# A graph network on Trainium2: 214 instead of 216 groups of tiles in each of three passes over the edges, with the last rounds of some loops written out

## What is computed

```python
def _propagate(h, edge_attr, edge_index, We, be, Wl):       # twice: pass 1 and pass 2
    x_edge = jnp.concatenate([h[edge_index[0]], h[edge_index[1]], edge_attr], axis=-1)
    x_edge = silu(x_edge @ We + be)
    x_edge = edge_attr @ Wl * x_edge
    return _seg_mean(x_edge, edge_index[0], h.shape[0]) + h

# layer 4: pass 3, with src = edge_index[0], dst = edge_index[1]
x_i, x_j = h[src], h[dst] + ee
alpha = leaky_relu((x_i * att_i).sum(-1) + (x_j * att_j).sum(-1))
e = jnp.exp(alpha - segment_max(alpha, src)[src])
alpha = e / (segment_sum(e, src)[src] + 1e-16)
out = segment_sum(x_j * alpha[:, :, None], src).mean(axis=1) + bias
```

## Time and profile before

| | us |
|---|---|
| median of 3 runs | 13832.53 |
| lowest and highest run | 13831.42, 13838.11 |
| the profiled execution | 13845.22 |
| its span, first to last instruction | 13843.5 |
| stage of pass 1, from the span's start | 6580 to 8870 |
| stage of pass 2 | 9050 to 11320 |
| stage of pass 3 | 11410 to 13720 |

### The profile page before, as it was taken

How to read it: one execution, slowest core, us unless ns; L and a number is a source line. 1 busy time by engine, 2 the same in 40 slices (tenths; PEclk the granted TensorE clock), 3 DMA queues, 4 the chain that set the end, 5 groups by cost and what they waited for, 6 DMA issues and landing times.

```text
span 13843.5 us, 199525 instructions
## 1 busy us (share of the span) xinstructions
PE 9124.3 (66%) x43992; PEld 6407.8 (46%) x43993; DVE 7459.0 (54%) x18791; ACT 3827.0 (28%) x8556; POOL 9553.0 (69%) x8478
## 2 busy tenths in 40 slices
PE   0266665776663679897666666766666656667676
PEld 0011112222111345554666666466666655666666
DVE  8876665777761220101343333333343348999998
ACT  0144445444410111111222222222222222333332
POOL 0168887888886766564777777467777757777774
PEclk9999999999996779898555555555555555665665
DMA  9942222222226999799644444244444438999996
GB/s 380 406 90 19 20 19 14 20 20 20 20 14 216 379 354 324 278 325 219 110 106 104 103 103 104 54 97 104 104 105 104 104 82 171 178 177 177 177 179 128
DMA packets 1476698, 1975.29 MB, mean 143 GB/s; under 512 B 1005691, under 2 KB 1023803, under 8 KB 1410045
## 3 DMA queue, kind: packets, MB, share of 16 engines
q1 hardware_dynamic: 744700, 1265.08, 34.4%
q0 software_dynamic: 454160, 346.91, 14.8%
q10 hardware_dynamic: 277362, 357.67, 8.1%
HBM read 1466.26 MB, written 503.63 MB: 142 GB/s over the span
## 4 chain that ended last, share of the span: by engine, by line
POOL 41%; issue 20%; DMA 13%; PE 11%; SPq 7%; DVE 6%; ACT 1%; DVEq 1%; POOLq 0%; ACTq 0%
POOL gat L793 24%; POOL adj L745 14%; DMA b_row<-acc 5%; PE bank L1230 4%; DMA adj<-put_n,put_at 4%; POOL rec_src L731 4%; SPq L684 3%; DMA arena<-adj 2%; SPq L691 2%; DMA rec_src<-pay,ring_i 2%; DVE arena L1585 1%; PE same L1374 1%; PE bank L1118 1%; SPq L679 1%; PE same L1165 1%
## 5 line engine op out<-in xcount | busy, mean ns | idle before, releaser
L793 POOL DMA_INDIRECT gat<-q_table,ring_i x3456 | 3482.4, 1008 | 1368.9 <-issue 1051.5
L745 POOL DMA_INDIRECT adj<-put_n,put_at x1632 | 2558.5, 1568 | 1276.2 <-DVE put_at L1669 660.1
L1396 PE MATMUL bank<-onehot_t,onehot 128*128 128x64 f32 x6912 | 1585.0, 424 | 1424.8 <-DVE acc L1887 973.6
L731 POOL DMA_INDIRECT rec_src<-pay,ring_i x1632 | 1740.1, 1066 | 866.9 <-issue 491.3
L1396 PEld LDWEIGHTS bank<-onehot_t,onehot 128*128 128x128 f32 x6912 | 1507.1, 331 | 1501.7 <-DVE acc L1887 850.9
L793 POOL DMA_INDIRECT arena<-h_table,ring_i x1728 | 1753.6, 1015 | 629.4 <-issue 503.3
L1300 PE MATMUL same<-onehot 32*128 32x512 f16 x3264 | 1680.0, 616 | 620.7 <-DVE onehot L1640 392.8
L1648 DVE TENSOR_SCALAR_CACHE_REDUCE onehot<-same 128x128 bf16<-128x128 f32 (+3 forms) x1632 | 1232.6, 755 | 867.0 <-PE same L1302 816.4
L1386 PE MATMUL bank<-hs,arena 128*128 x6912 | 1565.3, 422 | 89.7 <-ACT arena L1020 89.6
L1386 PEld LDWEIGHTS bank<-hs,arena 128*128 128x128 f32 x6912 | 1525.9, 334 | 92.8 <-issue 92.8
L902 ACT ACTIVATE arena<-iota_lo,arena 128x128 bf16<-128x128 f32 x3264 | 995.8, 387 | 1109.3 <-PE bank L1125 1009.2
(11 more groups left out here) (321 smaller groups left out, 13965.8 us busy)
## 6 DMA issues: line engine op xcount, KB each, us to landing
arena<-adj SPq DMA_DIRECT2D x240, 1280.0 KB
arena<-rec_src SPq DMA_DIRECT2D x3456, 69.0 KB
adj<-hs ACTq DMA_DIRECT2D x25, 6656.0 KB, 46.4
arena<-adj SPq DMA_DIRECT2D x60, 2560.0 KB, 18.1
rec_src<-pay ACTq DMA_DIRECT2D x1, 119232.0 KB, 332.3
arena<-lo_row SPq DMA_DIRECT2D x3456, 32.0 KB
hs<-b_row SPq DMA_DIRECT2D x432, 256.0 KB
acc<-b_row SPq DMA_DIRECT2D x432, 256.0 KB
```

The costliest lines, as they stand in the source:

```text
L731: nc.gpsimd.indirect_dma_start(rec_src, bass.IndirectOffsetOnAxis(ring_i[:, q, u:u + 1], 0), pay[:, q, u, :], None, bounds_check=SLOTS - 1 ...
L745: nc.gpsimd.indirect_dma_start(counts, bass.IndirectOffsetOnAxis(put_at[:, b // 3 % 4, c:c + 1], 0), put_n[:, b // 3 % 4, c:c + 1], None, ...
L793: nc.gpsimd.indirect_dma_start(rows[n][:, u, :], None, table, bass.IndirectOffsetOnAxis(ring_i[:, n, u:u + 1], 0)).then_inc(landed[n], 16)
L1396: last = mm(bank[6 + n % 2][:, u // 2 * D:(u // 2 + 1) * D], onehot[:, n % 2, u, :], msg[n % 2][:, u, :], start=u % 2 == 0, stop=u % 2 == 1)
```

## The change

`NL = 214` is the number of groups that can hold a tile below 1708. All engines stop after group 213 in each pass, and the counts that waits compare with follow: `k * NL` groups of pass 1, and `turns(n)`, the number of groups that used buffer `n`, 54, 54, 53 and 53. `NG`, the memory layout and the tables stay at 216 groups.

The last round no longer has all its groups: two of four in passes 1 and 2 (`REST4`), six of eight in pass 3 (`REST8`). POOL and SP end their loops a round earlier and run these behind the loop as straight code. DVE in passes 1 and 2 ends its loop a round earlier too, and writes out the last full round and the two groups behind it. In pass 3 the sums of the last group, which stood behind the last round on DVE, are now made in it, in the place of the first group that is left out.

```diff
--- before.py
+++ after.py
@@ -35,6 +35,8 @@
 E1, L1 = 10, 10 + D
 RW = 10 + 2 * D
 NG = TT // U
+NL = -(-TMAX // U)
+REST4, REST8 = NL - (NG // 4 - 1) * 4, NL - (NG // 8 - 1) * 8
 OFF = 4
 SPLIT = 8
 TA = 4 * P
@@ -60,6 +62,7 @@
 TQ = TT // 4
 PAIRS = U // 2
 HI_BITS = 6
+assert 0 < REST4 <= 4 and 0 < REST8 < 8 and NL % 2 == 0
 assert FA < FB and 4 * U * (FB + 1) <= TA < TT and NG % 4 == 0
 assert NG % 8 == 0 and NH <= 1 << HI_BITS and PAIRS * HI_BITS <= 24 and TQ <= 512
 PW = HEADS * D + 2 * HEADS
@@ -464,7 +467,7 @@
 
         def live(i, n):
 
-            return not isinstance(i, int) or 0 <= i * 8 + n < NG
+            return not isinstance(i, int) or 0 <= i * 8 + n < NL
 
         def eights(eng, body):
 
@@ -475,6 +478,10 @@
                     body(i, n)
             for n in range(8):
                 body(NG // 8 - 1, n)
+
+        def turns(n):
+
+            return (NL - n + 3) // 4
 
         def nth(i, n, lag=LAG):
 
@@ -640,24 +647,29 @@
             def load_all_edges(k):
                 if k:
                     sp.wait_ge(f_res, NCH * 4)
-                    sp.wait_ge(l_msg, NG + OFF)
-                    sp.wait_ge(l_oht, NG + OFF)
+                    sp.wait_ge(l_msg, NL + OFF)
+                    sp.wait_ge(l_oht, NL + OFF)
                 for n in range(4):
                     load_edges(k, 0, n)
+
+                def freed(i, n):
+                    sp.wait_ge(l_msg, i * 4 + (k * NL + n - 3 + OFF))
+                    sp.wait_ge(l_oht, i * 4 + (k * NL + n - 3 + OFF))
+                    load_edges(k, i, n)
 
                 def more(first, end):
                     with loop(sp, first, end) as i:
                         for n in range(4):
-                            sp.wait_ge(l_msg, i * 4 + (k * NG + n - 3 + OFF))
-                            sp.wait_ge(l_oht, i * 4 + (k * NG + n - 3 + OFF))
-                            load_edges(k, i, n)
+                            freed(i, n)
 
                 if k:
-                    more(1, NG // 4)
+                    more(1, NG // 4 - 1)
                 else:
                     more(1, FB)
                     store_other_digits()
-                    more(FB, NG // 4)
+                    more(FB, NG // 4 - 1)
+                for n in range(REST4):
+                    freed(NG // 4 - 1, n)
 
             store_table(EV_PQ, q_table[0], acc[:])
             store_first_digits()
@@ -795,16 +807,18 @@
                         bass.IndirectOffsetOnAxis(ring_i[:, n, u:u + 1], 0)).then_inc(landed[n], 16)
 
             def node_rows(k, i, n):
-                hold(pool, l_idx, i * 4 + (k * NG + n + 1))
+                hold(pool, l_idx, i * 4 + (k * NL + n + 1))
                 gathers(q_table[k], gat4, l_gat, n)
 
             for k in range(2):
                 pool.wait_ge(d_table, 16 * (1 + k))
                 for n in range(4):
                     node_rows(k, 0, n)
-                with loop(pool, 1, NG // 4) as i:
+                with loop(pool, 1, NG // 4 - 1) as i:
                     for n in range(4):
                         node_rows(k, i, n)
+                for n in range(REST4):
+                    node_rows(k, NG // 4 - 1, n)
 
             def score_rows(i, n):
                 hold(pool, t_idx, nth(i, n))
@@ -813,9 +827,11 @@
             pool.wait_ge(d_table, 16 * 3)
             for n in range(8):
                 score_rows(0, n)
-            with loop(pool, 1, NG // 8) as i:
+            with loop(pool, 1, NG // 8 - 1) as i:
                 for n in range(8):
                     score_rows(i, n)
+            for n in range(REST8):
+                score_rows(NG // 8 - 1, n)
 
 
         @block.scalar
@@ -1008,10 +1024,10 @@
                                    bias=b_mlp[m][:, 0:1]).then_inc(f_act, 1)
 
             def propagate_act(k):
-                G = k * NG
+                G = k * NL
 
                 def distance(i, n):
-                    act.wait_ge(l_lo[n], i * (16 * SPLIT) + (k * (NG // 4) + 1) * 16 * SPLIT)
+                    act.wait_ge(l_lo[n], i * (16 * SPLIT) + (k * turns(n) + 1) * 16 * SPLIT)
                     act.activation(lo_bc[n], lo_bc[n], ACT.Abs, bias=neg_p[:, 0:1]).then_inc(l_abs, 1)
 
                 def onehot_rows(i, n):
@@ -1047,8 +1063,8 @@
                     for b in range(1, 4):
                         digit_rows(b)
                     groups(FA, NG // 4 - 1)
-                for n in range(4):
-                    group(NG // 4 - 1, n, 4 - n)
+                for n in range(REST4):
+                    group(NG // 4 - 1, n, REST4 - n)
 
             layer_act(0, "h", FT[1])
             digit_rows(0)
@@ -1413,8 +1429,8 @@
                     for b in range(1, 4):
                         digit_rows(b)
                     groups(FA, NG // 4 - 1)
-                for n in range(4):
-                    if n < 3:
+                for n in range(REST4):
+                    if n < REST4 - 1:
                         look_up(NG // 4 - 1, n + 1)
                     sums(NG // 4 - 1, n)
 
@@ -1861,9 +1877,9 @@
                     last.then_inc(l_oh, 1)
 
                 def edge_part(i, n):
-                    landed = i * (16 * U) + (k * (NG // 4) * 16 * U + 16 * U)
+                    landed = i * (16 * U) + (k * turns(n) * 16 * U + 16 * U)
                     dve.wait_ge(l_gat[n], landed)
-                    dve.wait_ge(l_pay[n], i * (16 * SPLIT) + (k * (NG // 4) + 1) * 16 * SPLIT)
+                    dve.wait_ge(l_pay[n], i * (16 * SPLIT) + (k * turns(n) + 1) * 16 * SPLIT)
                     v.tensor_tensor(gat4[n], gat4[n], pay4[n][:, :, E1:E1 + D], ALU.add).then_inc(l_q1, 1)
 
                 def node_part(i, n):
@@ -1911,14 +1927,16 @@
                             group(i, n)
 
                 if k:
-                    groups(1, NG // 4 - 1)
+                    groups(1, NG // 4 - 2)
                 else:
                     groups(1, FB)
                     dve.wait_ge(d_tab[1], 16)
-                    groups(FB, NG // 4 - 1)
+                    groups(FB, NG // 4 - 2)
                 for n in range(4):
-                    group(NG // 4 - 1, n, more=False, last=n == 3)
-                gather_sums(NG // 4 - 1, 3)
+                    group(NG // 4 - 2, n, more=n < REST4)
+                for n in range(REST4):
+                    group(NG // 4 - 1, n, more=False, last=n == REST4 - 1)
+                gather_sums(NG // 4 - 1, REST4 - 1)
 
             def residual(j, n, other):
                 for c, (c0_, m) in enumerate(CHUNKS):
@@ -2127,10 +2145,7 @@
                     onehot_columns(i, n + 1)
 
             eights(dve, scores)
-            his = sums_ready(NG // 8 - 1, 7)
-            for k in range(PAIRS * HEADS):
-                bucket_sum(NG // 8 - 1, 7, his, k)
-            dve.wait_ge(t_add, (NG + LAG) * 8)
+            dve.wait_ge(t_add, (NL + LAG) * 8)
 
             parts = sums.rearrange("p n (h w) -> p n h w", h=HEADS)
             do(v.tensor_scalar(rden[:], parts[:, :, :, LH - 1], 1e-16, None, ALU.add))
```

## The result

The changed kernel takes 13768.23 us (median of 5 runs, 13744.97 to 13778.82) against 13832.53 us (5 runs, 13820.89 to 13841.29); the ratio is 0.995 with a 95% interval of 0.9935 to 0.9965. It is faster, by some 64 us. 13770.4 us were forecast, a ratio of 0.9955.

What follows compares the result with a forecast made beforehand. POOL's gathers were taken to bound passes 1 and 2, DVE pass 3. Removed groups 63.1 us less seams 1.0 gave 62.1 us: 13832.5 to 13770.4 us, range 13766 to 13779, 8 in 10 for 13762 to 13783.

Steps and rivals of the forecast that it cites:

- The bound: POOL's eight gathers per group pace passes 1 and 2 (10.54, 10.49 us); DVE's reduction paces pass 3 (10.70 us).
- The removed groups: Two groups fewer per pass at about interior price: 21.1, 21.0 and 21.0 us, together 63.1 us less.
- the 243 us of that rival: Forecast for 208 groups if padding is cheaper: 9.96 us a group in passes 1 and 2, 10.43 in pass 3.
- The slow gather: Passes 1 and 2: one gather per group takes 1.25 us, not 0.94, while DVE runs two-input L1859; goes with its group.
- The seams: POOL's loop exits into straight code in passes 1 and 2: 0.5 us each, 1.0 us lost; bounds 0 and 1.7.
- The covers that I named for SP and DVE: Slack hiding a 0.85 us code halt in passes 1 and 2: 2.6 us for SP, 2.5 us for DVE's index; cost 0.
- The stages between the passes: Stages outside the three passes; no term in the sum, taken as unchanged.
- what would make the prediction wrong: Signs: a pass's group price changes, POOL idles over 1 us at the seam, or stages between passes get longer.
- Lost loops: Rival (b): loop bodies halt for code each round, 129 rounds, 110 us lost; 48 us slower, 13880; chance 0.02.
- Seams: Rival (a): up to two 0.85 us code halts at each of seven loop exits, 12 us; gain 51, 13781; chance 0.08.
- Cheaper groups: Rival (c): groups worth only their end place, 60.5 us, 1 to 5 covered; gain 55 to 60, 13775; chance 0.15.

Runs made afterwards that it cites:

- the fastest kernel that serves any input: Changed kernel with one-hot columns of passes 1 and 2 written by eight 128x128 single-input instructions, not two of 128x512; 13608.77 us, ratio 0.982 to the kernel before.

## Why the prediction was right

**The bound.** Right. POOL paces passes 1 and 2, DVE pass 3, and no pass changed its pace by more than profiles of one kernel differ.

**The removed groups** (21.1, 21.0 and 21.0 us). Right within what can be told: 39 us timed for passes 1 and 2, 19 for pass 3, and 248 for 24 groups where the same prices give 254. That padding is not cheaper is only shown roughly, as the 243 us of that rival are inside the interval too. One reading beneath it was not right: the groups at the end were said to be shorter because SP has no more to load. In the profile of before POOL's gaps there are 0.30 us as everywhere, and the gathers of the last two groups of pass 1 were held for 0.18 and 0.03 us in all, where the mean group has 0.52. In the second profile of the changed kernel the last two groups of pass 1 have no such relief (0.77 and 0.74 us). So the shorter end is a matter of what the gathers meet on DVE, and nothing shows SP in it.

**The slow gather.** The rule was right and my reading of it too simple. It is not one for each group, but the gathers that start while certain DVE instructions are in flight with over 0.13 us left (L1859, L1867, L1877), 1.6 in a group, 0.55 us together. The sum did not depend on it, since the price was taken from whole groups.

**The seams** (1.0 us). Mis-sized by 1 us: POOL's gap was 0.30 us, the seams cost it 0. The covers that I named for SP and DVE held or were not needed; they were not tested one by one. The range around the forecast was added up 1 us too low at its lower end: 13831.4 - 64.0 is 13767, not 13766.

**The stages between the passes.** I put them at no change. That is where the profile of the changed kernel departed, by 8 us, and what would make the prediction wrong named only stages that get longer, not shorter. By that sign the stage ahead of pass 3 speaks against the prediction, as it got 1.5 us longer in the first pair; its other profiles have 102.1 us before and 101.9 and 101.8 after, so this is scatter. The length of PE's stretch at full clock is a term that one profile cannot give.

**The scatter.** The sum came from one profile whose passes ran at 10.51 and 10.49 us; the other profiles with this DVE code had 10.48 to 10.61. This makes single spans differ by 10 to 20 us a pass, so the agreement of 42.5 with 42.1 in the first pair is partly luck. What stands is the timed ratio: forecast 0.9955, measured 0.995 twice. Whether some of it is the longer stretch at full clock between the passes is not shown.

**Rivals.** Lost loops: out, by the ratio and by the silent code queues. Seams: 12 us are not excluded by the timed runs, but POOL has no halt in passes 1 and 2. Cheaper groups: not excluded, 60.5 and 63.1 us can't be told apart here.

## What to carry to other kernels

When work is taken out of a stage, its worth is the time from one group to the next on the engine that paces the stage, not the busy time of what goes. Ask what makes that engine's instructions differ in length: here half a microsecond of each group was another engine's doing, and cutting DVE's instructions finer, at more DVE time, gave about two to two and a half times what the change gave. And look into the trace even when the size comes true: the fastest kernel that serves any input was built on a theory that its own trace refutes. Before a difference of some microseconds between two profiles is explained, take a second profile of each.

## What was not expected of the hardware

- A gather of 128 rows that POOL starts while DVE has an instruction with two SBUF inputs in flight waits for what is left of it less 0.13 us: 0.35 us on average for 128x512 f32 (152 of 152 cases of L1859, 58 of 77 of L1867), 0.14 for 128x256. It is not held if it starts within 0.045 us of such an instruction (19 cases of L1867).
- Instructions of DVE with a single input differ: the 128x2048 reduction (256 cases) held none, but the 128x128 `tensor_scalar` held 103 of 179, by the same rule, these by 0.07 us on average and 0.12 at most. Instructions with one input in PSUM (184 cases) held none.
- After 2.3 ms at half clock, PE's granted clock rose for 17.1 (the kernel with 128x256 pieces), 20.5 or 30.7 us in the layers behind pass 1, with 20.5 and 30.7 in two executions of one kernel. A layer takes 11.15 or 20.75 us by it, the stage 144, some 142 or 134 us.
- A loop of POOL that ends in straight code cost nothing at the exit here, 0.30 us as between any two gathers (in all three passes of the changed kernel), where DVE had 0.85 us at its exit in pass 3.
